# A convolution and attention-like chain on one core: weight sums moved to GpSimd, one of its products moved to ScalarE, the other tied to VectorE's steps, and a new order at the start and the end

## The reference

```python
t1 = p1_w * x;  t2 = x + t1;  t4 = relu(x)
t5 = unfold(x, 3, 7, pad 1, 3)                       # 21 shifted copies of x
t7 = einsum('oc,nchw->nohw', p7_w, t4)
t8 = unfold(t7, 1, 5, dilation 3, pad 6)             # 5 shifted copies along a row
t9 = x[:, :, None] - t8
t10 = einsum('ngihw,goi->ngohw', t2 in groups, p10_w in groups)
t11 = einsum('nck,nmk->ncm', t1, t5) / sqrt(h * w)
t12 = t9.mean(2)
t13 = einsum('ncm,nmk->nck', t11, t10) / sqrt(c * 21)
out = maximum(t13, t12)
```

## Time and profile before

| what | value |
|---|---|
| median of 3 runs | 444.5 us (443.45 to 449.87) |
| profiled execution, its own time | 445.76 us |
| span of the profile | 443.8 us (1.96 us lie around it) |
| TensorE (PE) matmuls busy | 410.6 us, 93% |
| VectorE (DVE) busy | 374.6 us, 84% |
| ScalarE (ACT) busy | 190.5 us, 43% |
| GpSimd (POOL) busy | 161.7 us, 36% |
| granted clock of TensorE, mean | 0.979 of full |

### The profile page before, as it was taken

The page is one execution under the profiler, slowest core; times in us unless marked ns, Lnnn a source line. Parts: engine busy times, 40 slices in busy tenths (PEclk is TensorE's granted clock), DMA queues, the critical chain, the costliest instruction groups (busy, mean ns, idle before and its releaser), DMA issues.

```text
span 443.8 us, 12111 instructions
## 1 busy us (share of the span) xinstructions
PE 410.6 (93%) x5122; PEld 260.3 (59%) x5122; DVE 374.6 (84%) x406; ACT 190.5 (43%) x462; POOL 161.7 (36%) x101
## 2 busy tenths in 40 slices
PE   4956999999998999989999999989999899989996
PEld 1311567566765668756753568756786468746453
DVE  7799896988889887897869989898889988795824
ACT  1404462545343551545525453435525354345820
POOL 0295003911168221921129311762219311560100
PEclk9969999999999999989999999999999999999999
DMA  8931336355383644644554454836555443712105
GB/s 315 406 150 55 104 104 204 139 171 167 119 313 75 224 153 132 235 152 149 151 174 170 151 177 132 309 84 219 153 174 191 150 151 98 261 52 92 65 10 189
DMA packets 24100, 72.36 MB, mean 163 GB/s; under 512 B 2800, under 2 KB 3056, under 8 KB 24048
## 3 DMA queue, kind: packets, MB, share of 16 engines
q1 hardware_dynamic: 24048, 71.61, 48.0%
HBM read 54.82 MB, written 16.78 MB: 161 GB/s over the span
## 4 chain that ended last, share of the span: by engine, by line
PE 65%; DVE 20%; issue 9%; ACT 3%; DMA 1%; DVEq 0%; ACTq 0%; SPq 0%
PE ps_y L530 32%; PE ps_y L542 15%; PE ps_t L542 10%; PE ps_p L542 8%; DVE pair_sum L418 4%; DVE v_planes L389 3%; DVE yT L408 3%; DVE v_planes L387 2%; DVE base L451 2%; DVE v_planes L379 2%; DVE ps_y L397 2%; ACT q_sb L229 1%; ACT base L229 1%; DMA xw<-x_conv 1%; DVE box L426 1%
## 5 line engine op out<-in xcount | busy, mean ns | idle before, releaser
L530 PE MATMUL ps_y<-v_planes,u_planes 64*64 64x512 f32 x2048 | 298.6, 606 | 12.8 <-DVE ps_y L399 8.8
L530 PEld LDWEIGHTS ps_y<-v_planes,u_planes 64*64 64x64 f32 x2048 | 139.9, 136 | 108.4 <-issue 45.4
L205 POOL TENSOR_TENSOR t1T<-t1T,p1T_sb 128x512 f32<-128x512 f32 x64 | 100.8, 1610 | 104.2 <-DMA t1T<-x_pix 104.2
L542 PE MATMUL ps_t<-t,aT 64*64 64x512 f32 x456 | 123.0, 605 | 11.7 <-DVE base L451 10.7
L542 PE MATMUL ps_p<-box,p_fifth 64*64 64x512 f32 x480 | 126.6, 593 | 0.1
L214 POOL TENSOR_TENSOR t<-xn,p_plus 128x512 f32<-128x512 f32 x32 | 60.3, 1889 | 143.9 <-PE ps_t L542 143.9
L229 ACT ACTIVATE base<-ps_p 128x512 f32<-128x512 f32 x60 | 35.8, 597 | 170.7 <-PE ps_p L542 170.7
L284 ACT ACTIVATE t<-xn,p_plus 128x64 f32<-128x64 f32 x256 | 64.2, 333 | 0.0
L542 PE MATMUL ps_y<-t1T,yT 64*64 64x128 f32 x2048 | 60.3, 270 | 2.0 <-issue 1.6
L542 PEld LDWEIGHTS ps_y<-t1T,yT 64*64 64x64 f32 x2048 | 57.4, 133 | 7.0 <-DVE yT L408 3.9
L451 DVE TENSOR_TENSOR base<-ps_t,base 128x512 f32<-128x512 f32 x57 | 38.9, 683 | 16.7 <-PE ps_t L542 16.7
(11 more groups left out here) (30 smaller groups left out, 125.2 us busy)
## 6 DMA issues: line engine op xcount, KB each, us to landing
xw<-x_conv SPq DMA_DIRECT2D x32, 594.0 KB, 5.7
xn<-x_nat SPq DMA_DIRECT2D x32, 512.0 KB, 4.8
t1T<-x_pix SPq DMA_DIRECT2D x32, 512.0 KB, 6.2
out<-base SPq DMA_DIRECT2D x64, 256.0 KB, 2.4
u_planes<-w_tiles SPq DMA_DIRECT2D x4, 384.0 KB, 5.9
p1T_sb<-p1T SPq DMA_DIRECT2D x1, 128.0 KB, 6.3
p_sb<-p7T SPq DMA_DIRECT2D x1, 64.0 KB, 6.1
p_sb<-p SPq DMA_DIRECT2D x1, 32.0 KB, 6.3
```

Of the source, the lines that this page charges most:

```text
L205: nc.gpsimd.tensor_tensor(part, part, p1T_sb[:, e, :].unsqueeze(1).broadcast_to([P, 4, C]), ALU.mult).then_inc(t1_ready, 1)
L530: last = nc.tensor.matmul(dst[TILE * pair:TILE * pair + TILE, :], u_planes[rows, u % GROUPS, weights, TILE * k:TILE * k + TILE], v_planes[ ...
L542: last = nc.tensor.matmul(dst[cols, 0:data.shape[-1]], weights[rows, cols], data[rows, :], start=start, stop=False, skip_group_check=True)
```

## The change

1. TensorE runs three matmuls of zeros at the start (`WARM = 3`).
2. `weights(g)` for g = 1 to 3 goes to GpSimd, as one sum and, after ScalarE has halved both the plane `U_2` and the sum (`half_sums`, new), an add and a subtract. `u_sum` has a place for each group. `p7_fifth` and the first `copy_two` come behind these on ScalarE.
3. VectorE's first image has a list of its own: planes(1) before seeds(0), planes(2) and seeds(1) before box_sums(0, 0), and box sums of quarters 1 and 2 around seeds(2) and seeds(3).
4. GpSimd's `t1_part` waits for VectorE's box steps: three parts after box_fours(n, 1), three after box_pairs(n, 2), two after box_last(n, 2). It has no t2 any more.
5. ScalarE makes all t2 halves; those of odd h stand behind `copy_two` in each block. `load_natural` waits for one semaphore `t2_ready`.
6. At the end: `zero_three(31)` is woven between the halves of the outputs, `y_times_t1(7)` is cut in three with p7 products between, banks are given out differently, and t13 of the last image waits for its own banks only (`bank_free`) instead of for all base halves. VectorE runs box_pairs(7, 3) ahead of turn_y(31). ScalarE makes t2 halves 5 to 7 ahead of base halves 5 to 7, and `first_part_of_a` ahead of base half 7 alone.

```diff
+WARM = 3
-        u_sum = sb("u_sum", [P, 2, WCOLS])
+        u_sum = sb("u_sum", [P, GROUPS, WCOLS])
-        tail_p7 = {3: ps_y[2][0], 4: ps_y[2][1], 6: ps_y[0][0], 7: ps_y[0][1]}
-        tail_t13 = [ps_t13, ps_p7, ps_y[2][0], ps_y[2][1], ps_y[0][0], ps_y[0][1], ps_y[1][0], ps_y[1][1]]
+        tail_p7 = {3: ps_y[2][0], 4: ps_y[2][1], 6: ps_t13, 7: ps_y[0][1]}
+        tail_t13 = [ps_y[0][0], ps_y[2][0], ps_y[2][1], ps_y[1][0], ps_y[1][1], ps_p7, ps_t13, ps_y[0][1]]
...
             def load_natural(n, f):
-                wait(sp, t2_even, 4 * (n - 1) + f + 1)
-                wait(sp, t2_odd, 4 * (n - 1) + f + 1)
+                wait(sp, t2_ready, 8 * (n - 1) + 2 * f + 2)
...
+            def weights(g):      # on GpSimd
+                pool.wait_ge(w_loaded[g], 16)
+                nc.gpsimd.tensor_tensor(u_sum[:, g, :], u_planes[:, g, U_0, :], u_planes[:, g, U_3, :],
+                                        ALU.add).then_inc(u_later, 1)
+                pool.wait_ge(half_ready, 2 * g + 1)
+                nc.gpsimd.tensor_tensor(u_planes[:, g, U_1, :], u_sum[:, g, :], u_planes[:, g, U_2, :],
+                                        ALU.add).then_inc(u_later, 1)
+                pool.wait_ge(u_later, U_STEPS * (g - 1) + 2)
+                nc.gpsimd.tensor_tensor(u_planes[:, g, U_2, :], u_sum[:, g, :], u_planes[:, g, U_2, :],
+                                        ALU.subtract).then_inc(u_later, 1)
+
+            for g in range(1, GROUPS):
+                weights(g)
...
             for n in range(N_IMG):
-                for q in range(8):
+                pool.wait_ge(box_steps, BOX_STEPS * (4 * n + 1) + 2)
+                for q in range(3):
                     t1_part(n, q)
-                for h in range(1, 8, 2):
-                    t2_half(n, h)
+                pool.wait_ge(box_steps, BOX_STEPS * (4 * n + 2) + 1)
+                for q in range(3, 6):
+                    t1_part(n, q)
+                pool.wait_ge(box_steps, BOX_STEPS * (4 * n + 2) + 3)
+                for q in range(6, 8):
+                    t1_part(n, q)
...
+            def half_sums(g):
+                act.wait_ge(u_later, U_STEPS * (g - 1) + 1)
+                copy(u_sum[:, g, :], u_sum[:, g, :], 0.5).then_inc(half_ready, 1)
...
-            for g in range(2):
+            half_weights(0)
+            for g in range(1, GROUPS):
                 half_weights(g)
+                half_sums(g)
             act.wait_ge(small_loaded, SMALL)
             copy(p7_fifth[:], p7_sb[:], FIFTH).then_inc(p7_scaled, 1)
-            for g in range(2, GROUPS):
-                half_weights(g)
...
                 copy_two(u)
+                t2_half(n - 1, 3)
...
                 copy_two(u + 1)
+                t2_half(n - 1, 5)
...
                 copy_two(u + 2)
+                t2_half(n - 1, 7)
...
                 copy_two(u + 3)
+                t2_half(n, 1)
             seed_x(LAST, 3)
             seed_x(LAST, 4)
             relu(LAST, 3)
             t2_half(LAST, 2)
             base_half(LAST, 2)
+            seed_x(LAST, 5)
             base_half(LAST, 3)
-            seed_x(LAST, 5)
+            t2_half(LAST, 3)
             seed_x(LAST, 6)
             seed_x(LAST, 7)
             t2_half(LAST, 4)
             base_half(LAST, 4)
-            t2_half(LAST, 6)
+            for h in range(5, 8):
+                t2_half(LAST, h)
+            base_half(LAST, 5)
+            base_half(LAST, 6)
             first_part_of_a(LAST)
-            for h in range(5, 8):
-                base_half(LAST, h)
+            base_half(LAST, 7)
...
             weights(0)
             planes_low(0)
             planes_high(0)
-            weights(1)
-            for n in range(N_IMG):
+            planes_low(1)
+            planes_high(1)
+            seeds(0)
+            planes_low(2)
+            planes_high(2)
+            seeds(1)
+            box_sums(0, 0)
+            turn_y(0)
+            planes_low(3)
+            planes_high(3)
+            seeds(2)
+            box_pairs(0, 1)
+            box_fours(0, 1)
+            turn_y(1)
+            planes_low(4)
+            planes_high(4)
+            seeds(3)
+            box_last(0, 1)
+            box_pairs(0, 2)
+            for n in range(1, N_IMG):
...
+            box_pairs(LAST, 3)
             turn_y(UNITS - 1)
+            box_fours(LAST, 3)
+            box_last(LAST, 3)
             max_half(LAST - 1, 7)
-            box_sums(LAST, 3)
...
+            for _ in range(WARM - 1):
+                nc.tensor.matmul(ps_p7[:], zeros[:, 0:P], zeros[:, 0:HALF], start=True, stop=True)
...
+            outputs_first(p_a, t_a, done + 3)
+            zero_three(UNITS - 1, True, 0)
+            outputs_second(p_a, t_a, done + 3)
+            zero_three(UNITS - 1, True, 1)
+            outputs_first(p_b, t_b, done + 4)
+            zero_three(UNITS - 1, False, 0)
+            outputs_second(p_b, t_b, done + 4)
+            zero_three(UNITS - 1, False, 1)
+            outputs_first(p_c, t_c, done + 5)
+            outputs_second(p_c, t_c, done + 5)
+            y_times_t1(LAST, 0, BLOCKS)
             p7_rows(LAST, 5, 0)
             p7_rows(LAST, 6, 0).then_inc(item_half, 1)
+            y_times_t1(LAST, BLOCKS, BLOCKS + 8)
             pe.wait_ge(item_half, done + 6)
             p7_rows(LAST, 5, 1).then_inc(p7_done, 1)
             p7_rows(LAST, 7, 0).then_inc(item_half, 1)
+            y_times_t1(LAST, BLOCKS + 8, 2 * BLOCKS)
             pe.wait_ge(item_half, done + 7)
             p7_rows(LAST, 6, 1).then_inc(p7_done, 1)
             p7_rows(LAST, 7, 1).then_inc(p7_done, 1)
+            def bank_free(h):
+                held = {1: 3, 2: 4, 5: 5, 6: 6, 7: 7}.get(h)
+                if held is not None:
+                    pe.wait_ge(base_ready, 8 * LAST + held + 1)
+                else:
+                    pe.wait_ge(out_ready, 8 * LAST)
             def last_first(h):
-                pe.wait_ge(base_ready, 8 * LAST + 8)
+                bank_free(h)
+                bank_free(h + 1)
```

More of the change, by code:

```diff
@@ L84, in t13_bank @@
         def t13_bank(n, h):
-            return tail_t13[h] if n == LAST else ps_t13
+            if n == LAST:
+                return tail_t13[h]
+            return ps_y[0][0] if (n, h) == (LAST - 1, 7) else ps_t13
         def a_banks(n):
@@ L262, in seed_x @@
                     act.wait_ge(base_ready, 8 * n + 3)
+                elif h == 6:
+                    act.wait_ge(out_ready, 8 * n - 1)
                 else:
@@ L285, in t2_half @@
                                                 scale=p1_plus[:, 8 * h + r:8 * h + r + 1])
-                last.then_inc(t2_even, 1)
+                last.then_inc(t2_ready, 1)
             def first_part_of_a(n):
@@ L474, in _ @@
                 seeds(u)
-                if n == 0:
-                    weights(2)
                 turn_y(u - 1)
@@ L486, in _ @@
                 seeds(u + 1)
-                if n == 0:
-                    weights(3)
                 turn_y(u)
@@ L589, in zero_three, with y_times_t1 @@
                         last.then_inc(m_done, 1)
-            def y_times_t1(n):
+            def y_times_t1(n, tiles_from=0, tiles_to=2 * BLOCKS):
                 if n < 0:
                     return
-                pe.wait_ge(y_turned, 8 * n + 8)
-                pe.wait_ge(t1_ready, 8 * n + 8)
-                for t in range(2 * BLOCKS):
+                if tiles_from == 0:
+                    pe.wait_ge(y_turned, 8 * n + 8)
+                    pe.wait_ge(t1_ready, 8 * n + 8)
+                for t in range(tiles_from, tiles_to):
                     e, j = t // BLOCKS, t % BLOCKS
@@ L600, in y_times_t1 @@
                         last = half_product(a_banks(n)[half], yT[:, e, j, :], t1T[:, e, j, :], half, t == 0)
-                last.then_inc(a_done, 1)
+                if tiles_to == 2 * BLOCKS:
+                    last.then_inc(a_done, 1)
             def p7_rows(n, h, half):
@@ L614, in t13_rows @@
                     pe.wait_ge(aT_ready, n + 1)
-                    pe.wait_ge(t2_odd if h % 2 else t2_even, 4 * n + h // 2 + 1)
+                    pe.wait_ge(t2_ready, 8 * n + h + 1)
                     if n < LAST:
-                        wait(pe, out_ready, 8 * n + h)
+                        wait(pe, out_ready, 8 * n + h - (t13_bank(n, h) is not ps_t13))
+                    if (n, h) == (LAST - 1, 7):
+                        pe.wait_ge(y_turned, 2 * (UNITS - 1))
                 return half_product(t13_bank(n, h), aT[:, n % 2, :], t2[:, h, :], half, first)
@@ L668, in _ @@
             done = 8 * LAST
-            slot(UNITS, (LAST, 2), (LAST - 1, 5), (LAST, 3), (LAST - 1, 6))
-            outputs_first((LAST, 4), (LAST - 1, 7), done + 5)
-            outputs_second((LAST, 4), (LAST - 1, 7), done + 5)
-            y_times_t1(LAST)
+            p_a, t_a, p_b, t_b, p_c, t_c = ((LAST, 2), (LAST - 1, 5), (LAST, 3), (LAST - 1, 6), (LAST, 4), (LAST - 1, 7))
+            outputs_first(p_a, t_a, done + 3)
```

(2 more changed lines are left out.)

30 lines of the change are left out of this document (11 added, 19 removed).

## The result

The changed kernel takes 423.79 us (median of 4 runs, 422.5 to 425.3) where the kernel before takes 445.77 (4 runs, 443.45 to 449.87): a ratio of 0.952, 95% interval 0.947 to 0.956. The profiled execution took 423.14 us, its span is 421.3. From span to span 22.5 us are gone: 443.8 less 421.3.

What follows compares the result with a forecast made beforehand. TensorE, busy 93% of the span, was taken as the bound, its idle and low-clock time as the possible gain. Images 12.4, start 6.3 and end 1.5 sum to 20.2 us: 425.6, stated as a median of 425.0, range 416 to 437.

Steps and rivals of the forecast that it cites:

- the maximum at 346.38: VectorE's late maximum in an image: reading PSUM, it keeps its 0.68 us, taken as PSUM work being free beside GpSimd.
- SBUF — State Buffer: Skill section on ports: VectorE and GpSimd share an exclusively locked port pair, met by VectorE only with two SBUF inputs.
- The size of the images' gain: Images: 12.4 us forecast, from 10.7 us of waits for VectorE's maximum and 1.7 us of lower clock; ends 0 and 12.4.
- 1.94 us are idle: exactly one wait: One late image: of 50.60 us, matmuls are busy 48.66; TensorE's idle rest is one wait for VectorE's maximum.
- The idle term: Images: TensorE's waits for VectorE's maximum of an output half all go, 10.7 us in 7 pieces.
- 1.7 (clock): Images: the lowered clock behind one wait goes too, a quarter of 6.6 us, 1.7 us gained.
- 0.4 us of idle forecast: ScalarE, ahead of the base half behind relu: the added t2 half's 2.0 us fit into 2.37 us of idle.
- a new wait of near 5 us for box_last: Start, slot 4: p7 of quarter 1 wants box_last(0, 1), so TensorE idles 37.5 to 42.4, 4.9 us.
- TensorE never waits for VectorE from 16.9 to 37.5: Start, slots 1 to 3: TensorE runs without waits, 6.9 + 6.9 + 8.6 us less what is done ahead.
- The chain's sum: Start, GpSimd weights to the first q_sb copy: seven instructions of 0.9 us plus two ScalarE handoffs, put at 8.3 us.
- GpSimd's weights hold the start up: Rival, start: weight instructions take 1.6 us each beside VectorE's planes, q_sb is late, start gains 0 to 1: 431; chance 0.14.
- two drains of TensorE's pipe, 0.5 us each: End: weaving zero_three with the outputs takes these pauses away, 1.0 us gained.

Runs made afterwards that it cites:

- e1: The changed kernel without GpSimd's three waits for box steps, all t2 halves staying on ScalarE: 436.8 us, ratio 0.981 to the kernel before.
- e3: The changed kernel with GpSimd's old list per image, eight unpaced t1 parts then t2 of odd halves: 444.5 us, ratio 0.998 to the kernel before.
- e14: The changed kernel with three extra 128x512 copies on ScalarE ahead of each odd t2 half of images 0 to 6: 443.1 us, ratio 0.999.
- e2: The changed kernel with t2 of odd halves back on GpSimd, the pacing kept: 423.1 us, ratio 0.951 to the kernel before.
- e8: The changed kernel with four more matmuls of zeros into an unused bank ahead of zero_three(0): 421.5 us, ratio 0.943 to the kernel before.
- e4: The changed kernel with copy_two(0) moved on ScalarE ahead of the halvings of groups 2 and 3: 417.2 us, ratio 0.939.
- e12: The changed kernel with the whole start of the kernel before; pacing, t2 on ScalarE and end stay new: 417.5 us, ratio 0.935.
- e13: The changed kernel with the end of the kernel before, all t2 halves still on ScalarE: 422.4 us, ratio 0.948 to the kernel before.
- e9: The changed kernel with weight sums of groups 1 to 3 back on VectorE and ScalarE's old prelude: 418.4 us, ratio 0.938.

## Why the prediction was right, point by point

The time, 425.0 against 423.8, came out better than its terms: the start was put 4.0 us too high and the images 6.1 too low. That these two errors nearly cancel is luck. (The base also moved: the kernel before had a median of 444.5 when the forecast was made and has 445.77 beside the result. And 425.6 less the 1.3 us named there is 424.3, not 425.0.)

*What bounds it; the pacing.* Right, and shown: the meetings of GpSimd's t1 with VectorE made the wait (e1, e3), the three groups fit beside PSUM work in the images, and an image lost its one wait. One reading is wrong, though what it says holds: the maximum at 346.38 does not show that PSUM work keeps its time beside GpSimd, since GpSimd stood idle from 345.38 to 349.57. One that does ran beside the t1 parts of the earlier trace rows:

```profile
338.60 0.68 DVE L451 TENSOR_TENSOR base<-ps_t,base 128x512 f32<-128x512 f32 x1
```

The prediction also gave the rule of the Trainium skill's "SBUF — State Buffer" (section "Who interferes with whom") too short: besides two SBUF inputs the page names VectorE's 2-port performance modes. Every VectorE instruction that was slowed in the rows shown has two SBUF inputs.

*The size of the images' gain.* The step that was mis-sized is "1.94 us are idle: exactly one wait", with 48.66 us of busy time taken as what must remain. The idle term itself was good: 12.6 less 2.2 is 10.4 us, for 10.7. But busy time fell by 9.1 us as well, of which only 1.7 (clock) and 1.0 (drains at the end) had been forecast. 3.4 of the 9.1 are clock: two of the seven stretches before had a mean clock of 0.97 (1.7 us each; the prediction counted one), and after the change all seven have 1.00. The other 5.7 come to 0.8 us an image. (Second clock stretch and these 5.7, less 0.3 of idle and 1.0 of drains that did not come, are the 6.1.) `q_sb` of the kernel before marks its blocks:

```profile
333.09 0.58 ACT L229 ACTIVATE q_sb<-ps_y 128x512 f32<-128x512 f32 x1
...
343.50 0.58 ACT L229 ACTIVATE q_sb<-ps_y 128x512 f32<-128x512 f32 x1
...
356.44 0.58 ACT L229 ACTIVATE q_sb<-ps_y 128x512 f32<-128x512 f32 x1
```

The block with the wait takes 12.94 us; the next one, to 366.74 in the earlier trace rows, takes 10.30, the usual length. So 2.6 are lost, 1.94 of them idle. In e1_unpaced such a block takes 12.01 (285.30 to 297.31), 1.7 lost with 0.71 idle. The other 0.7 to 1.0 us are busy by the profile. The matmuls of t13 that wait use one row half of the array and otherwise alternate with those of p7 on the other; here all four of p7 stand alone ahead of the wait:

```profile
344.25 1.02 PE L542 MATMUL ps_p<-box,p_fifth 64*64 64x512 f32 x4
```

That t13 then runs without its partner, and that this is the 0.8 us, is argued from the rows; no run isolates it.

*ScalarE.* 0.4 us of idle forecast, 0.46 to 0.47 measured; e14 finds 1.3 us of slack in a block, for 1.2. That t2 has to leave GpSimd, which the prediction took for granted, fell with e2.

*The start.* The order of events was right (`q_sb` at 15.0 forecast, 15.62 measured; a new wait of near 5 us for box_last: 4.22, from 42.2 on). The step that failed is "TensorE never waits for VectorE from 16.9 to 37.5": it took units 1 and 2 at full clock although 4 us of idle stood ahead of them, while it charged such an idle at slot 4 with 2.1 us. Of the 4.0 us, 2.8 are this clock (the rows at e8), and 0.8 came ahead of it (seeds(0) done at 17.73 for 16.9). GpSimd's nine weight instructions took 0.72 to 0.73 alone and 0.93 to 1.72 beside planes, 0.98 in the mean, for the 0.9 taken; the seven on the chain to the copy have a mean of 1.06. The chain's sum is not clear as written (7 x 0.9 and two handoffs of 1.4 make 9.1, not 8.3); measured it is 8.5, from 6.53 to 15.06.

The rival "GpSimd's weights hold the start up" was right in that TensorE idles past the copy with the clock down, but not in its price (1.6 us for each instruction) nor its gain of 0 to 1 (2.3). Its rule, in the Trainium skill's "GPSIMD Engine Reference", section 4.1 (two-input elementwise work belongs on VectorE, since GpSimd is about twice as slow), fits the price in this trace, 0.72 us alone for 0.42 on VectorE. It does not explain the loss: e4 wins it back with the sums still on GpSimd. And the prediction never asked what the pacing would do for the old start; e12 shows 8.8 us there.

*The end.* 1.5 us forecast, nothing measurable found (e13). The "two drains of TensorE's pipe, 0.5 us each" are shown by no run: with the old order the stretch that should hold them is no longer than with the new one.

## What to carry to other kernels

Where two engines slow each other in SBUF work, tie the freer one to steps of the busier one that are followed by work from PSUM; here three semaphore waits gave nearly the whole gain, and with them in place the work moved from GpSimd to ScalarE gave nothing. A chain that opens the pipeline (here the first `q_sb`) should stand ahead of all preparation that is needed later, and idle ahead of it is paid twice when TensorE's clock falls. When an edit has several parts, time the old form of each with the rest kept, and where one old form undoes two things (e9), split it (e4). Of the six parts here the fourth carries nearly the whole gain, the second hides a loss of 5 us, and the other four give nothing that can be measured.

## What was not expected of the hardware

- A block in which t13 waits costs 0.7 to 1.0 us more than the idle that the profile shows (above); in e14_act_more a wait for a seed shown as about 0.2 us goes with 0.53 us of loss in its block.
- Matmuls of zeros kept the granted clock up through an idle stretch (e8: 1.00, against a mean of 0.61 or 0.81 behind 4.0 us of idle in two runs of the same start).
- TensorE pauses by 0.2 to 1.4 us (2.5 in e14_act_more) inside y_times_t1, put down by the profile to "issue", 0.3 to 3.7 us in all for a run (9.5 in e14_act_more), in differing images; images of one run differ by up to 1.1 us (48.19 to 49.30 in the changed kernel, where the longest pause is 0.69). Its cause stays open.
